# Three neighbouring batches run in one list-scheduled order, with q, k, v and the attention outputs passed through DRAM

## The reference, cut to what matters

```python
x = x + _layernorm(attn(_layernorm(x), Wq, Wk, Wv, Wo))
x = x + _layernorm(moe(_layernorm(x), gate_w, gate_up, down, shared...))
# attn: q, k, v = x@Wq, x@Wk, x@Wv; rope(q), rope(k)
#       probs = softmax(where(causal, q@k.T / 4, -max)); out = (probs@v)@Wo
# moe:  top 6 of softmax(x@gate_w.T); routed rows are scattered to
#       buf_tok[64, 128], silu(g)*u, down, weighted, added back; plus shared expert
```

## Time and profile before

| what | us |
|---|---|
| median of 3 runs | 2284.23 |
| lowest, highest | 2275.66, 2322.41 |
| profiled execution, span from first to last instruction | 2301.7 |
| the four batches in it, to the experts' start | 1838 |
| experts | 374 |
| final normalisation | 90 |

### The profile page before, as it was taken

How to read it: one execution, slowest core, us unless ns; L and a number is a source line. 1 busy time by engine, 2 the same in 40 slices (tenths; PEclk the granted TensorE clock), 3 DMA queues, 4 the chain that set the end, 5 groups by cost and what they waited for, 6 DMA issues and landing times.

```text
span 2301.7 us, 41702 instructions
## 1 busy us (share of the span) xinstructions
PE 1964.9 (85%) x12707; PEld 976.5 (42%) x12707; DVE 1314.6 (57%) x2831; ACT 1042.5 (45%) x1568; POOL 718.4 (31%) x985
## 2 busy tenths in 40 slices
PE   6999979989999799889997979899979688998930
PEld 3434335544333355543343545334345344444410
DVE  4588836546798265468982654688736312222248
ACT  2557753334677433446774334567733222222200
POOL 2212214522222145222222452122215422222248
PEclk9889989987899899979998999799989899999975
DMA  2122323310000121100001110000002199999988
GB/s 84 55 93 94 127 87 111 137 54 2 11 16 12 33 98 67 38 6 11 12 12 42 62 59 21 6 12 12 16 28 75 62 300 322 335 335 315 339 252 293
DMA packets 108130, 232.81 MB, mean 101 GB/s; under 512 B 24423, under 2 KB 24423, under 8 KB 107920
## 3 DMA queue, kind: packets, MB, share of 16 engines
q1 hardware_dynamic: 81072, 191.07, 23.9%
q0 software_dynamic: 24576, 35.07, 6.3%
q10 hardware_dynamic: 2272, 4.06, 0.5%
HBM read 141.59 MB, written 126.48 MB: 116 GB/s over the span
## 4 chain that ended last, share of the span: by engine, by line
PE 59%; DVE 12%; issue 10%; DMA 7%; ACT 3%; POOL 2%; DVEq 2%; SPq 1%; another core or an unknown queue 1%; POOLq 1%; ACTq 0%
PE ps L759 9%; DVE rmax L1212 8%; PE ps L698 7%; PE ps L653 6%; DMA gx<-dispatch_scratch 6%; PE ps L898 5%; PE ps L845 4%; PE ps L779 4%; PE ps L871 3%; PE ps L930 3%; PE ps L884 3%; PE ps L654 3%; PE ps L673 2%; PE ps L872 2%; PE ps L705 2%
## 5 line engine op out<-in xcount | busy, mean ns | idle before, releaser
L1212 DVE TENSOR_REDUCE rmax<-ps 128x1 f32<-128x512 f32 (+3 forms) x1280 | 732.5, 632 | 188.0 <-PE ps L708 114.2
L1038 ACT ACTIVATE pr<-ps 128x1024 f32<-128x1024 f32 (+3 forms) x768 | 586.2, 813 | 239.4 <-PE ps L779 233.2
L698 PE MATMUL ps<-kT,qT 48*128 48x512 f16 (+3 forms) x1536 | 396.5, 349 | 34.0 <-DVE rmax L1212 23.8
L759 PE MATMUL ps<-pr,v_ones 128*32 128x512 f32 (+3 forms) x3072 | 348.1, 528 | 7.9 <-POOL pr L1488 4.5
L1488 POOL TENSOR_SCALAR_AFFINE_SELECT pr<-pr 128x512 f32<-128x512 f32 x256 | 162.2, 638 | 502.5 <-ACT pr L1038 501.1
L779 PE MATMUL ps<-qT,kT 50*128 50x512 f16 (+3 forms) x1536 | 301.4, 344 | 17.0 <-ACT pr L1038 7.9
L698 PEld LDWEIGHTS ps<-kT,qT 48*128 48x128 f16 x1536 | 123.3, 95 | 343.8 <-DVE rmax L1212 282.8
L1534 POOL DMA_INDIRECT dispatch_scratch<-x,slot_i x192 | 190.1, 990 | 73.4 <-issue 73.4
L705 PE MATMUL ps<-above,sel 64*128 64x128 bf16 x1024 | 190.1, 227 | 0.0
L898 PE MATMUL ps<-gu_sb,gxT 128*128 128x384 f32 x512 | 189.0, 493 | 0.0
L1553 POOL DMA_INDIRECT acc_scratch<-eo,etok x64 | 98.7, 1541 | 282.5 <-DVE eo L1351 270.3
(11 more groups left out here) (149 smaller groups left out, 2599.0 us busy)
## 6 DMA issues: line engine op xcount, KB each, us to landing
gu_sb<-w_gu_dram SPq DMA_DIRECT2D x64, 768.0 KB, 7.6
dn_sb<-w_dn_dram SPq DMA_DIRECT2D x64, 384.0 KB, 9.0
dispatch_scratch<-blank SPq DMA_DIRECT2D x8, 2308.0 KB, 8.8
gx<-dispatch_scratch SPq DMA_DIRECT2D x64, 288.5 KB, 5.2
xin<-x_dram SPq DMA_DIRECT2D x32, 256.0 KB
acc_scratch<-blank SPq DMA_DIRECT2D x32, 256.0 KB, 2.1
xres<-x_dram SPq DMA_DIRECT2D x32, 256.0 KB
x_scratch<-x SPq DMA_DIRECT2D x32, 256.0 KB, 2.0
```

The lines of the kernel that those rows point to most:

```text
L698: last = pe.matmul(o, qT[r:r + SROWS, half, 2 * g + h // 2, q % QPH * P:(q % QPH + 1) * P], kT[r:r + SROWS, g, kh * HALF:kh * HALF + w], s ...
L759: last = pe.matmul(ps[32 * h:32 * h + 32, 6, c0:HALF], v_ones[g % 2][:, kt, :], pr[i % SLOTS][:, h, 0:HALF - c0], start=kt == 0, stop=kt = ...
L1038: act.activation(pr[i % SLOTS][:, 2 * pair:2 * pair + 2, 0:HALF - c0], ps[:, 2 + 2 * pair:4 + 2 * pair, 0:HALF - c0], ACT.Exp, scale=facto ...
L1212: dve.tensor_reduce(dst[:, heads[0] % 2, heads[0] // 2:heads[0] // 2 + n, q % QPH], ps[:, BANK_OF[item], 0:n * w].rearrange("p (h k) -> p ...
```

## The change

The loops over batches and their phases go. A class `Plan` lists every operation of the whole part before the experts (per tile, per group, per unit) in streams, each with its engine, an assumed duration, an aim (in batches) and what it must follow. It walks time forward: of the next operations of all streams it takes the one that can start first, by aim where equal, and so writes one order for each engine. Each engine then issues its list, unrolled. The aims put the projections of batch b+1 and the final stage of batch b-1 beside the attention of batch b. The experts and the final normalisation stay as they were.

With it come these edits:
- The rotation moves from VectorE, which read PSUM, to GpSimd. ScalarE copies the projection to SBUF first (`copy_qkv`, two operations per tile, 480 and 288 columns). The rotated q, k and v of a tile are stored to DRAM and loaded per group (`store_rotated`, `load_group`: 1024 pieces of 384 bytes). The weights' columns are reordered so that a group is contiguous.
- High and low parts, stacks and their transposes are made per group and not per tile, with `qT` and `kT` for two groups.
- `raw` is transposed and divided right after each half group, and stored to DRAM (pieces of 256 bytes); the final stage loads it per tile.
- The output projection is copied out of PSUM by ScalarE (`copy_wo`) before VectorE normalises it. Gate and up of the shared expert are separate units of 384 columns.
- Everything but the transposed scores and the outputs takes its PSUM bank from the same three, 0, 1 and 7; banks 2 to 6 join when attention is over.
- The weights of the final stage are loaded at the start, and the slots are cleared in 64 smaller DMAs.

```diff
+SHARED_BANKS = (0, 1, 7)
+LATE_BANKS = (2, 3, 4, 5, 6)
+class Plan:
...
+        for n in range(nt):
+            b, t = divmod(n, TT)
+            at = b - 1 + 0.06 + 0.70 * (t + 1) / TT if b else -1 + 0.1 * t
...
+                    op(s_qk, ("qk", n, part, c), "pe", w / 600 + 0.01, at - 0.10 + 0.012 * (4 * part + c), ("xtc", n),
+                       bank=("q", n, part) if c == 0 else None)
...
+            op(s_rot, ("rot", n), "pool", 4.9, at + 0.02, ("qe", n, 1))
+            op(s_rs, ("rs", n), "sp", 0.06, at + 0.03, ("rot", n))
...
+        for gi in range(NG):
+            b, g = divmod(gi, KVH)
+            at = gi / KVH
+            far = gi - 2
+            op(s_gl, ("gl", gi), "sp", 0.1, at - 2.6 / KVH, *[("rs", TT * b + t) for t in range(TT)],
...
+        for n in range(nt):
+            b, t = divmod(n, TT)
+            at = b + 1 + 0.03 + 0.9 * t / TT
+            e = 1 / 300
...
+    def run(self):
...
+                if name in self.takes_bank:
+                    if not free_at:
+                        continue
+                    bank = min(free_at, key=lambda k: (max(at, free_at[k]), -free_at[k]))
+                    at = max(at, free_at[bank])
+                key = (at, self.aim[name])
+                if best is None or key < best[0]:
+                    best = (key, i, name, bank)
...
+            def rotate(n):
...
+                pool.tensor_tensor(rot_a[:], qk, cos, ALU.mult)
+                pool.tensor_tensor(rb2[:, :, :, :, 0], qk2[:, :, :, :, 1], sn, ALU.mult)
+                pool.tensor_tensor(rb2[:, :, :, :, 1], qk2[:, :, :, :, 0], sp_, ALU.mult)
+                pool.drain()
+                pool.tensor_tensor(qk, rot_a[:], rot_b[:], ALU.add).then_inc(rot_ready, 1)
...
+            for what in PLAN.order["pool"]:
```

More of the change, by code:

```diff
@@ new lines, in program @@
+        rmax = [sb(f"rmax{k}", [P, 48], f32, att) for k in range(2)]
+        nm = sb("nm", [P, 16], f32, att)
+        mb = [sb(f"mb{k}", [P, 32], f16, att) for k in range(2)]
+        mT = [sb(f"mT{k}", [32, P], f16, att) for k in range(2)]
+        pr = [sb(f"pr{k}", [P, REP, HALF], f32, att) for k in range(SLOTS)]
+        raw = [sb(f"raw{k}", [P, HALF], f32, att) for k in range(2)]
+        rden = sb("rden", [P, QPH * REP], f32, att)
+        an_g = [sb(f"an_g{k}", [P, QPH, REP * HD], f32, att) for k in range(2)]
@@ new lines, in score @@
+            def score(gi, u):
+                half, q, kh, w, heads = UNITS[u]
+                if u == 0:
+                    pe.wait_ge(stack_copied, 3 * gi + 3)
+                free_bank(("u", gi, u))
+                diag = q // QPH == kh
+                for k, h in enumerate(heads):
+                    r = ROWT * (h % 2)
+                    o = ps[:, bank_of["u", gi, u], k * w:(k + 1) * w]
+                    last = pe.matmul(o, qT[gi % 2][r:r + SROWS, half, h // 2, q % QPH * P:(q % QPH + 1) * P],
+                                     kT[gi % 2][r:r + SROWS, kh * HALF:kh * HALF + w], start=True, stop=not diag)
+                    if diag:
+                        pe.matmul(o[:, w - P:w], sel[r:r + ROWT, 0, :], above[r:r + ROWT, r:r + P],
+                                  start=False, stop=False)
+                        last = pe.matmul(o[:, w - ROWT:w], sel[r:r + ROWT, 1, :], above[r:r + ROWT, r:r + ROWT],
+                                         start=False, stop=True)
+                last.then_inc(sc_done, 1)
@@ new lines, in outputs @@
+            def outputs(gi, i):
+                qh, kt, c0 = PUNITS[i]
+                pe.wait_ge(exp_done, 2 * NP * gi + 2 * i + 2)
+                if DIAG[i]:
+                    pe.wait_ge(masked, NDIAG * gi + sum(DIAG[:i + 1]))
+                if i == 0:
+                    pe.wait_ge(v_ready, gi + 1)
+                    if gi:
+                        pe.wait_ge(pv_copied, 2 * gi)
+                if i == HALF1:
+                    pe.wait_ge(pv_copied, 2 * gi + 1)
+                for h in range(REP):
+                    last = pe.matmul(ps[32 * h:32 * h + 32, 6, c0:HALF], v_ones[gi % 2][:, kt, :],
+                                     pr[(NP * gi + i) % SLOTS][:, h, 0:HALF - c0], start=kt == 0,
+                                     stop=kt == QPH * (qh + 1) - 1)
+                last.then_inc(pv_done, 1)
@@ L1334, in _ @@
-                end_phase(dve, b, 1)
-            end_late_phase(dve, 0)
+                    dve.max(top8[:], sc)
+                    dve.drain()
+                    dve.max_index(idx8[:], top8[:], sc)
+                elif part == 1:
+                    dve.drain()
+                    dve.tensor_copy(idxf[:], idx8[:, 0:TOPK])
+                    dve.drain()
+                    dve.tensor_tensor(onehot[:], iota_e[:].unsqueeze(1).broadcast_to((P, TOPK, E)),
+                                      idxf[:].unsqueeze(2).broadcast_to((P, TOPK, E)), ALU.is_equal)
+                else:
+                    dve.drain()
+                    if n:
+                        dve.wait_ge(pos_done, n)
+                    with nc.allow_low_precision("a sum of zeros and at most one 1"):
+                        dve.tensor_reduce(pick[:], onehot[:].rearrange("p k e -> p e k"), AX, ALU.add).then_inc(pick_ready, 1)
@@ L1551, in add_rows @@
+            for k in range(4):
+                wait_apart(pool, sent[k], 16 * TOPK * (NT // 4))
+            end_phase(pool, 0)
             def add_rows(e, k):
```

1855 lines of the change are left out of this document (904 added, 951 removed).

## The result

| | median us | lowest to highest | runs |
|---|---|---|---|
| before | 2303.98 | 2275.66 to 2322.41 | 5 |
| changed kernel | 2383.56 | 2330.35 to 2385.99 | 5 |

The ratio is 1.030, its 95% interval 1.017 to 1.043; it is taken from the faster runs of each kernel, those within 1.5% of its fastest, while the medians of all five give 1.035. So the change makes the kernel slower, by 2 to 4%. The forecast was 1984, range 1870 to 2150. The profiled execution is the fastest of the five, 2330.35 us. Those medians go from 2286.90 to 2315.24, so two runs of different sessions are compared to some 30 us at best.

The account below looks back on a forecast made before the run. VectorE's maxima bound attention, TensorE's fp32 matmuls the other stages; fused batches would be TensorE-bound. 105 + 235 + 736 + 315 + 147 + 464 = 2002 us, 300 less than the profiled 2301.7; applied to the median, 1984, range 1870 to 2150.

Parts of the forecast that it names:

- The first exponential: Start of the kernel: preparation, projections and first group's loads, stacks and maxima end at 105 us, where it was 100.5.
- Batch 0: Attention of the first batch, with only some five projection tiles beside it, bound by VectorE: 235 us.
- Batches 1 and 2: Middle batches, holding projections, attention and final stage together, bound by TensorE: 368 us each.
- Batch 3: Last batch's attention, with a final stage but no projections beside it: 315 us.
- TensorE's work: TensorE's operations for a batch with all three stages, taken as the new bound: 320 us, ends 300 and 365.
- The fill of 0.87: Share of time TensorE would be filled where it bounds the fused batches, against 0.89 for VectorE in attention alone.
- The last final stage: Final stage of the last batch, alone after attention, costing what it did before: 147 us.
- the rest: Experts and last normalisation behind the batches, untouched by the change: 464 us.
- A: Fused batches: fuller queues, TensorE reaches 0.96 where it bounds; 1865 us as a median, chance 0.17.
- B: Attention: GpSimd's rotations and indirect DMAs delay masks, outputs and exponentials; half exposed, 2140 us as a median, chance 0.21.
- C: Hand-overs of three shared PSUM banks stop TensorE's list; fully exposed 547 us more, 2530 us, chance 0.08.
- D: Fused batches: fixed lists wait for each other, copies and loads eat what is hidden; about 2284 us, chance 0.04.

Follow-up runs that it names:

- e6: Changed kernel with ScalarE issuing the four loads of the final stage's weights only after the scales are ready; 2347.92 us.
- e4: Changed kernel's instructions reordered: planner charges for changes of array arrangement and has costs set nearer to the trace; 2249.08 us.
- e12: Changed kernel in its own order, two of four chunks of the shared expert's gate and up projections left out; 2353.82 us, ratio to before 1.026.
- e10: Changed kernel's instructions in an order found by searching the planner's numbers, judged by replaying its lists; 2204.78 us, ratio to before 0.960.
- e11: Changed kernel with a third buffer for stacked queries and keys, order found by a replay-judged search; 2130.36 us, ratio to before 0.931.
- e8: Changed kernel with GpSimd's rotation cut to one multiplication, order unchanged; 2356.69 us.
- e7: Changed kernel with two shared PSUM banks in place of three, lists planned anew; 2749.52 us.
- e1: Changed kernel with its phases kept apart again, all instructions and DRAM traffic kept; 2460.30 us.
- the control: Changed kernel itself, unedited, run again in a later session; 2362.68 us, ratio to before 1.028.

## Why the prediction was wrong

The side was wrong and the size by 400 us: 1984 against 2383.56. Of this, 327 stand in the profiled execution (2328.6 against 2002). The rest is that this execution is the fastest of its five runs, where that of before lay 17.5 us above its median. The forecast's own sign of being wrong, a fused batch of over 400 us, came; its other, VectorE or ScalarE busier than 0.9, did not (275 and 252 of 450).

- **The first exponential**, 105: came at 119.9, 15 us late. Preparation was taken as 3 us longer. TensorE waited until the weights were scanned, 26.8 us instead of 15.2, as the first row shows. The second shows what VectorE had waited for before its scan: the first loads, of which the rotary table came last. In e6 that wait was 1.3 us and TensorE's 16.7. But in e4, with the four loads where they were, TensorE's was 15.3, so the late weights aren't shown to be the cause.

```profile
PE ps L687 <- DVE wmax L1207: 26.8, 1, 26.8
...
DVE wmax L1205 <- DMA ropes_sb<-rope_s_dram: 11.5, 1, 11.5
```

- **Batch 0**, 235: took 296.6. **Batches 1 and 2**, 368 each: 451.7 and 450.8. **Batch 3**, 315: 398. This is 62 + 84 + 83 + 83 = 312 of the 327 us.
- **TensorE's work**, 320 us a batch, is the first half of the step that failed. As far as it went it was right: the list needs an estimated 1282 / 4 = 320.5 with no wait and no change of arrangement, and batch 1's share 326. But it put the changes of arrangement at nothing, and their 453 in batch 1 are 44 us more, 369.5 in all. At a fill of 0.87 this alone makes the batch 425 us and not 368. Rows of before could have shown it: 980 changes already stood in its loops.
- **The fill of 0.87** is the other half. I called it "my main choice" and carried it over from attention alone, where it was VectorE's. In batch 1 TensorE reached 369.5 / 451.7 = 0.82 with the changes counted, another 27 us, and 326 / 451.7 = 0.72 in the forecast's own terms. The clock alone, 0.94 in that window, is worth up to 27 us. I took the bounding engine's margin (320 against 273) as protection. e12 speaks against that: TensorE's work shrank by 62 us, and 10 came out. e4, e10 and e11 show that the loss hangs on the order, for with the same operations they are 107 to 239 us shorter in the stretch. e11 shows that 0.89 can be reached, though in a window without projections. So the figure was possible, but was a property of a good order and not of this one.
- **The groups' new work.** I counted stacks as work in the sum, not as a seam. With phases apart the path costs 32 us a batch (485 against 453), most of it in the six groups after the first, which take 31 us on average where they took 26.4.
- **The last final stage**, 147, and **the rest**, 464: 151 and 460. Right.
- **VectorE, ScalarE**: right for the fused batches, as shown above. GpSimd was 176 where 195 were forecast.

The rivals: A (0.96) didn't come. B, priced at 156, is refuted by e8 and by the 10.3 us that outputs waited for masks. C had the side, and e7 shows that its mechanism exists. At three banks the replay gives it some 40 us, which no run checks. Its sign, TensorE's waits above 300 us, can't decide: the weight loads of the scores wait 230 us for the maxima now, and waited 283 before. D, "fixed lists wait for each other as the phases do now", named the mechanism. I gave it 0.04 and no price of its own. With the new path's cost that e1 shows added, it would have been the slower case: 145 us paid, 77 to 98 won back.

Neither of the two rules weighed there shows in the trace. The Trainium skill, "ScalarE: Activation LUTs", section "What ACT_TABLE_LOAD costs", would have ScalarE lose a drain at each load. The trace doesn't agree: here is the row for the 24 loads that now stand in front of attention's exponentials, with 0.4 us of idle time before all of them together.

```profile
L1053 ACT ACT_TABLE_LOAD x24 | 30.8, 1283 | 0.4
```

The Trainium skill, "DMA: Bandwidth & Descriptors", section "Specifications", gives 512 bytes as the least piece at line rate. No price for smaller ones shows here: a group's load of 384 KB in pieces of 384 bytes landed in 3.5 us at the median. In the same part of the kernel 256 KB of x, in rows of 2 KB, took 2.8, which is less per microsecond. (The routed rows' 288.5 KB took 5.0, but among the experts, where the DMA engines are full.)

```profile
gx<-dispatch_scratch SPq DMA_DIRECT2D x64, 288.5 KB, 5.0
...
grp<-rotated_scratch SPq DMA_DIRECT2D x32, 384.0 KB, 3.5
xin<-x_dram SPq DMA_DIRECT2D x32, 256.0 KB, 2.8
```

## What to carry to other kernels

When phases are merged into one written-out order, sum the engines' work to see what could be won, but price the order itself by replaying its lists against each other with durations from a trace: here that gave -24, -75, -160 and -176 us where the chip gave -40, -114, -158 and -232, and 320 where it gave 387. It had the side each time, and missed what the order did to the clock. Before trusting a planner, compare its table of costs with the trace (four DMAs planned at 0.15 us took 2.7), and charge it for what it can't see, such as changing the array's arrangement. Ask separately what the data path that allows the overlap costs with no overlap: e1 was a one-line edit and told most of the story.

## What the runs showed of the hardware

- A change of TensorE's arrangement costs 0.09 to 0.12 us: 0.094 to 0.096 after work on the whole array, 0.091 to 0.094 after a pair of transposed scores, 0.108 to 0.117 after outputs, alike in the kernel before and after.
- The granted clock follows the seams. In e1 it is 1.00 in 240 to 250 us. In the seam, from 250 to 260, TensorE was busy 8.33 us and not 9.89, with no gap over 0.65 us, and from 258.8 us on the clock stood at half, for 3.4 us. So it went in the steady groups of that batch, each time 2 to 3 us after a group's first exponential, for 3.4 to 6.8 us. In e11 it stood at 1.00 from 1000 to 1336 us, with TensorE busy 330 of the 336. A bad order may so cost twice.
- With 62 us of TensorE's work left out beside attention, e12 had a lower clock there, 0.914 where the control had 0.931. Over the whole span it was 0.898 to 0.909 in its six runs and 0.910 to 0.922 in the control's.
- The arrival of the first weights varies by some 10 us between runs that load them alike (TensorE's wait for their scan was 15.3 us in e4, 19.6 in e8, 25.6 in the control), enough to hide the 12 us that e6 was after.
